# Two-expert mixture around linear attention: transpositions up to four items early in two PSUM banks, second products four items behind the first, bias and x sums behind the loop

## The chip, the cores and the metric

One core of one Trainium2 chip runs the whole program. Times are device microseconds of one execution. The kernel before took 328.78 us, the median of 3 runs (328.49 to 335.28).

## The reference

Input x is 2048 rows of 128 float32. The program computes

```
x = x + 0.5 * ffn(layernorm(x))
x = x + attention(layernorm(x))        # linear attention, 16 heads of 8, causal prefix sums
x = x + 0.5 * ffn(layernorm(x))

ffn(x):                                # 8 experts, 128 -> 512 -> 128, the best two per row
    logits = x @ Wg
    top_w, top_i = top_k(logits, 2);  top_w = softmax(top_w)
    for each expert i:
        h = gelu(x @ W1[i] + b1[i]);  out_i = h @ W2[i] + b2[i]
        results += weight_of_i_per_row * out_i
```

## The kernel before

All arithmetic on the matrices is float32. The program has three parts: a mixture of experts (pass f = 0), attention (tile by tile, 16 tiles of 128 rows), and a mixture again (pass f = 1). Each engine has its own instruction stream; semaphores order them. The change touches the mixture alone.

**Routing.** Each row has two (row, expert) pairs, 4096 in all. They are sorted by expert into 32 tiles (NL) of 128 slots. A tile that holds rows of two experts is worked on once for each, so there are at most NS = 32 + 8 - 1 = 39 "items". Tables in SBUF tell each item its tile (`place`), its expert (`expert_i`) and which lanes are its own (`own_item`).

**The expert loop.** For each item:

- POOL gathers the 128 rows of a tile from DRAM by an indirect DMA (line 411) into `xg`, which is the same memory as `y_back`. Gather n waits until transposition n - 6 is done (there are six semaphores, GATHERS). With a lag of 18 it scatters finished tiles to `y_rows` in DRAM (line 419) from the same queue: gather n, then scatter n - 18. Scatter i waits until item i + 7 is added up (`y_sb`).
- PE transposes the gathered rows (line 1090) into one PSUM bank, `xg_bank`; it waits for the gather and for ACT's copy of the transposition before. ACT copies it to SBUF (line 550) and clears the tile's sum (line 551).
- PE makes the first product (`hidden`, line 1072, 8 matmul instructions) of the expert's W1 and the turned rows into one of three banks. SP loads that expert's W1 and b1 (258 KB) into one of six buffers (WEIGHTS) once the item six before is done.
- DVE adds b1 (line 847) into one of three `h_pre`; ACT takes the GELU (line 558) into one of three `h_act`.
- PE makes the second product (`output`, line 1081, 8 matmul instructions) into one of three banks; it waits for the GELU and for DVE's sum of three items before. DVE adds it to the tile's sum for the lanes that are the item's own (line 859).

PE's order is written out by hand. Step i is: transposition i + 2, first product i + 1, (every second step) a register load of the next places, second product i - 1. PE's queue is in order, so each of these stands behind the one before. ACT's step i is: copy i + 2, clear, GELU i, and for 16 of the steps one diagonal of gate weights (line 561). DVE's step i is: bias add i, sum i - 2.

**Bias and x sums** (`mix_start`, lines 1111 and 1113). Four PSUM banks take, for four tiles each, the b2 of both experts by the row's weights (2 matmul instructions) and x itself through the identity (8). The one for c = 0 stands in PE's queue behind step 1, the other three behind the loop. Then the second product of the weighted rows (`mix`, line 1135) is added for each chunk as soon as SP has loaded it back from `y_rows`; DVE adds the row's other half into x (line 898).

In pass 0, DVE takes the moments of the new x behind this (line 892), and their variance goes through POOL (line 429) and DVE (lines 684 and 687) to ACT's first normalised tile of the attention (line 596).

Of the kernel before, what the change touches and what calls it, by code (L numbers as in the profile page):

```python
# [26 lines left out]
P = 128  # L27
# [10 lines left out]
def macaron_kernel(nc, x_d, xT_d, Wa, ba, Wg, W1b, W2, b2, out_d):  # L38
# [24 lines left out]
    PLACES = 2  # L63
    ITEM_STEPS = 21
    assert D == P and NS % RING == 0 and GATHERS % RING == 0 and WEIGHTS % RING == 0 and T & (T - 1) == 0

    with ExitStack() as ctx:
# [121 lines left out]
        h_act = sb("h_act", [P, RING, DF])  # L189
# [313 lines left out]
        def _(act):  # L503
            s = nc.scalar

            def ffn(f):
# [40 lines left out]
                def rows(n):  # L547

                    act.wait_ge(xg_ps, NL * f + n + 1)
                    s.copy(xgT[:, n * P:(n + 1) * P], xg_bank).then_inc(xg_sb, 1)  # L550
# [14 lines left out]
                step(0, 0)  # L565
                act.wait_ge(w_allT_ps, f + 1)
                s.copy(w_allT[:, :], w_allT_bank).then_inc(w_allT_sb, 1)
                step(1, 1)
                step(2, 2)
                act.wait_ge(half_ready, f + 1)  # L570
                for t in range(NT):
                    step(RING + t, t % RING)
                    weights(t)
                for i in range(RING + NT, NS):
                    step(i, i % RING, lead=(i + 2 < NL))
# [80 lines left out]
        def _(dve):  # L656
# [184 lines left out]
            def experts(f):  # L841
# [34 lines left out]
                for i in range(loops * WEIGHTS, NS + 2):  # L876
                    step(i, i % WEIGHTS)
# [95 lines left out]
        def _(pe):  # L973
# [70 lines left out]
            def experts(f):  # L1044
# [31 lines left out]
                def output(i, r):  # L1076
                    col = at[i][1]
                    pe.wait_ge(h_gelu, base + i + 1)
                    at_least(pe, y_sb, base + i - RING + 1)
                    for c in range(FC):  # L1080
                        last = mm(y_bank(r), h_act[:, r, c * P:(c + 1) * P], w2[:, bass.ds(col + c * P, P)],  # L1081
                                  start=(c == 0), stop=(c == FC - 1))
                    last.then_inc(y_ps, 1)

                def transposed_rows(n):

                    r = n % GATHERS
                    pe.wait_ge(gathered[r], 16 * (n // GATHERS + 1 + uses(r, GATHERS, NL) * f))
                    at_least(pe, xg_sb, NL * f + n)
                    pe.transpose(xg_bank, xg[:, n, :], ident[:, :]).then_inc(xg_ps, 1)  # L1090

                def step(i):

                    if i + 2 < NL:
                        transposed_rows(i + 2)
# [4 lines left out]
                    if i:  # L1100
                        output(i - 1, (i - 1) % RING)
# [17 lines left out]
                step(1)  # L1119
                if f == 0:  # L1120
# [159 lines left out]
```

## Time and profile before

| | us |
|---|---|
| median of 3 runs | 328.78 |
| lowest, highest | 328.49, 335.28 |
| span of the profiled execution | 363.5 |
| its own time | not given apart from the span |
| PE busy (matmuls) | 306.2 |
| PE weight loads busy | 253.4 |
| DVE busy | 206.9 |
| POOL busy | 192.9 |
| ACT busy | 152.1 |

The span runs from the first to the last instruction of one execution that the hardware profiler recorded. PE = matmul, PEld = its weight loads, DVE = VectorE, ACT = ScalarE, POOL = GpSimd, SP = SyncE. Matmul ends are modelled in it. "Remote", or "another core or an unknown queue", is what the profile writes where it can't name what ended a wait.

### The profile page before, as it was taken

How to read it: one execution, taken by the hardware profiler on the slowest of the kernel's cores; microseconds unless marked ns; L12 is line 12 of the kernel's file. 1: busy time of each engine (PE TensorE's matmuls, PEld its weight loads, DVE VectorE, ACT ScalarE, POOL GpSimd, SP SyncE). 2: the span in 40 equal slices, each digit the busy share in tenths (PEclk: the TensorE clock that was granted, in tenths of full speed). 3: DMA queues.
4: the chain of work that ended last, by engine and by line, in shares of the span. 5: the costliest groups of instructions: out<-in, count | busy, mean ns of one | idle time of the engine just before them, and what ended most of it. 6: DMA issues, size and time to landing. Idle time of an engine off the chain costs nothing.

```text
span 363.5 us, 7851 instructions
## 1 busy us (share of the span) xinstructions
PE 306.2 (84%) x2041; PEld 253.4 (70%) x2041; DVE 206.9 (57%) x558; ACT 152.1 (42%) x481; POOL 192.9 (53%) x246
## 2 busy tenths in 40 slices
PE   8785999686789986999999995868998577699975
PEld 6533899686779955566767763427998576699954
DVE  0896263423245416799999999992553323345504
ACT  1794475524244321434545551832664342343200
POOL 6056546666654531676677773236556665645610
PEclk9998999989899998999999998586999989989986
DMA  6937376445456116000000000236665543455156
GB/s 198 303 138 209 100 186 187 129 134 133 130 150 169 56 50 213 0 0 2 1 3 0 3 1 30 87 94 178 154 179 130 159 133 107 119 149 160 37 156 206
DMA packets 23557, 41.52 MB, mean 114 GB/s; under 512 B 4065, under 2 KB 6113, under 8 KB 23522
## 3 DMA queue, kind: packets, MB, share of 16 engines
q1 hardware_dynamic: 19426, 32.68, 32.0%
q0 software_dynamic: 4096, 8.40, 7.7%
q8 instruction: 19, 0.31, 0.3%
q14 instruction: 16, 0.13, 0.1%
HBM read 33.72 MB, written 7.34 MB: 113 GB/s over the span
## 4 chain that ended last, share of the span: by engine, by line
PE 47%; DVE 13%; another core or an unknown queue 12%; ACT 9%; issue 8%; DMA 7%; POOL 3%; SPq 0%; DVEq 0%; POOLq 0%; ACTq 0%
PE banks L1072 16%; PE banks L1081 14%; PE banks L1195 3%; DVE prod L927 3%; DVE local L931 3%; DMA y_back<-y_rows 3%; ACT h_act L558 2%; DMA y_back<-xn_rows,src_row 2%; PE banks L1090 2%; POOL kv L442 2%; PE banks L991 2%; PE banks L1135 2%; PE banks L980 2%; DMA y_rows<-y_back,pair_row 1%
## 5 line engine op out<-in xcount | busy, mean ns | idle before, releaser
L411 POOL DMA_INDIRECT y_back<-xn_rows,src_row x64 | 61.9, 967 | 61.6 <-issue 21.7
L1072 PE MATMUL banks<-rows_sb,w1b 128*128 x624 | 91.0, 292 | 1.2 <-issue 1.2
L847 DVE TENSOR_TENSOR h_pre<-banks,w1b 128x512 f32<-128x512 f32 x78 | 53.7, 688 | 64.3 <-PE banks L1072 41.6
L1081 PE MATMUL banks<-w,h_act 128*128 x624 | 85.4, 283 | 1.1 <-ACT h_act L558 1.1
L1072 PEld LDWEIGHTS banks<-rows_sb,w1b 128*128 128x128 f32 x624 | 82.3, 205 | 3.6 <-issue 1.9
L419 POOL DMA_INDIRECT y_rows<-y_back,pair_row x64 | 62.6, 978 | 39.8 <-DVE y_back L859 22.9
L1081 PEld LDWEIGHTS banks<-w,h_act 128*128 128x128 f32 x624 | 79.0, 199 | 1.3 <-issue 1.3
L558 ACT ACTIVATE h_act<-h_pre 128x512 f32<-128x512 f32 x78 | 48.7, 624 | 22.1 <-DVE h_pre L847 17.4
L859 DVE SCALAR_TENSOR_TENSOR y_back<-banks,own_item,y_back 128x128 f32 x78 | 27.4, 351 | 51.4 <-PE banks L1081 32.1
L550 ACT COPY rows_sb<-banks 128x128 f32<-128x128 f32 x64 | 16.8, 262 | 85.4 <-remote 54.2
L1090 PE MATMUL banks<-ident,y_back 128*128 128x128 f32 x64 | 19.3, 302 | 28.2 <-issue 12.3
L442 POOL TENSOR_TENSOR kv<-qk,vx 128x1024 f32<-128x1024 f32 x16 | 31.5, 1969 | 18.1 <-DVE qk L884 18.1
L1090 PEld LDWEIGHTS banks<-ident,y_back 128*128 128x128 f32 x64 | 9.8, 153 | 32.2 <-issue 25.2
L1195 PE MATMUL banks<-kv,tri 128*128 128x384 f32 x64 | 24.8, 509 | 2.3 <-POOL kv L442 2.3
L980 PE MATMUL banks<-blank 128*128 128x512 bf16 x65 | 23.2, 524 | 1.2 <-DVE blank L915 1.2
L927 DVE TENSOR_TENSOR prod<-banks,qk 128x1152 f32<-128x1152 f32 x16 | 21.6, 1351 | 2.0 <-PE banks L1199 1.4
L931 DVE TENSOR_REDUCE local<-prod 128x144 f32<-128x1152 f32 x16 | 21.6, 1353 | 0.6
L898 DVE SCALAR_TENSOR_TENSOR x<-y_back,half_w,banks 128x128 f32<-128x128 f32 x32 | 8.9, 342 | 20.3 <-PE banks L1135 11.3
L551 ACT ACTIVATE y_back<-ident 128x128 f32<-128x128 f32 x64 | 20.1, 314 | 0.0
L1195 PEld LDWEIGHTS banks<-kv,tri 128*128 128x128 f32 x64 | 10.9, 189 | 9.7 <-POOL kv L442 5.3
L1135 PE MATMUL banks<-y_back,diag 128*128 128x128 f32 x64 | 12.5, 372 | 5.3 <-DMA y_back<-y_rows 5.3
L980 PEld LDWEIGHTS banks<-blank 128*128 128x128 bf16 x65 | 7.7, 126 | 12.9 <-issue 8.4
(201 smaller groups left out, 427.1 us busy)
## 6 DMA issues: line engine op xcount, KB each, us to landing
w1b<-in_W1b SPq DMA_DIRECT2D x78, 258.0 KB
y_back<-y_rows SPq DMA_DIRECT2D x16, 256.0 KB, 5.6
xn_rows<-rows_sb SPq DMA_DIRECT2D x8, 256.0 KB, 2.3
rows_sb<-in_x_T SPq DMA_DIRECT2D x4, 256.0 KB, 4.0
x<-in_x_tiles SPq DMA_DIRECT2D x4, 256.0 KB, 6.2
y_back<-xn_rows,src_row POOLq DMA_INDIRECT x64
y_rows<-y_back,pair_row POOLq DMA_INDIRECT x64
out<-x SPq DMA_DIRECT2D x4, 256.0 KB, 2.3
```

Source lines behind the costliest of these rows:

```text
L411: g.indirect_dma_start(out=xg[:, n, :], out_offset=None, in_=xn_rows[f][:, :], in_offset=bass.IndirectOffsetOnAxis(ap=src_row[:, n:n + 1], ...
L419: g.indirect_dma_start(out=y_rows[f][:, :], out_offset=bass.IndirectOffsetOnAxis(ap=pair_row[:, i:i + 1], axis=0), in_=xg[:, i, :], in_off ...
L442: g.tensor_tensor(o4, k4, v4, ALU.mult).then_inc(kv_sb, 1)
L558: s.activation(h_act[:, r, :], h_pre[:, r, :], ACT.Gelu_apprx_tanh).then_inc(h_gelu, 1)
L847: v.tensor_tensor(h_pre[:, r, :].rearrange("p (c n) -> p c n", c=FC), h_bank(r).rearrange("p (c n) -> p c n", c=FC), w1b[:, q, DF:DF + FC] ...
L927: v.tensor_tensor(prod[:, :].rearrange("p (b e n) -> p b e n", b=3, n=P), prefix_bank.rearrange("p b (e n) -> p b e n", n=P), q4, ALU.mult ...
L931: v.tensor_reduce(local[:, :, :].rearrange("p e h -> p (e h)"), prod[:, :].rearrange("p (g d) -> p g d", d=DH), AX.X, ALU.add).then_inc(lo ...
L980: mm(banks[:, bank, :], blank[:, 0:P], blank[:, :], start=True, stop=True)
L1072: last = mm(h_bank(r)[:, c * P:(c + 1) * P], w1b[:, q, c * P:(c + 1) * P], xgT[:, bass.ds(at[i][0], P)], start=True, stop=True)
L1081: last = mm(y_bank(r), h_act[:, r, c * P:(c + 1) * P], w2[:, bass.ds(col + c * P, P)], start=(c == 0), stop=(c == FC - 1))
L1090: pe.transpose(xg_bank, xg[:, n, :], ident[:, :]).then_inc(xg_ps, 1)
L1195: mm(prefix_bank[:, b, :], tri[:, :], kv[:, r, b * n:(b + 1) * n, :].rearrange("p e n -> p (e n)"), start=True, stop=True)
```

## The change

The transpositions alternate between two PSUM banks (0 and 1). A function `turned(i)` says how many tiles are transposed by the end of step i: i + 3 as before, one more from step 3 and two more from step 6, at most 32. PE and ACT both follow it. The second product of item i - 3 stands in step i, where that of i - 1 stood; `h_act` has six buffers in place of three. DVE's sum moves from i - 2 to i - 4. The transposed gate weights move from bank 1 to bank 7. All four `mix_start` stand behind the last second product.

```diff
+    TURNS = 2
+    BEHIND = 3
+    AHEAD = 4
+    ACTS = 6
...
-        h_act = sb("h_act", [P, RING, DF])
+        h_act = sb("h_act", [P, ACTS, DF])
...
-        xg_bank = banks[:, 0, 0:P]
+        def xg_bank(n): return banks[:, n % TURNS, 0:P]
+        def turned(i):
+            return min(i + 3 + min(max(i, 0) // 3, AHEAD - 2), NL)
...
-        w_allT_bank = banks[:, 1, 0:P]
+        w_allT_bank = banks[:, 7, 0:P]
...
-                def step(i, r, lead=True):
-                    if lead:
-                        rows(i + 2)
+                def step(i):
+                    for n in range(turned(i - 1), turned(i)):
+                        rows(n)
                     act.wait_ge(h_biased, base + i + 1)
-                    at_least(act, y_ps, base + i - RING + 1)
-                    s.activation(h_act[:, r, :], h_pre[:, r, :], ACT.Gelu_apprx_tanh).then_inc(h_gelu, 1)
+                    at_least(act, y_ps, base + i - ACTS + 1)
+                    s.activation(h_act[:, i % ACTS, :], h_pre[:, i % RING, :], ACT.Gelu_apprx_tanh).then_inc(h_gelu, 1)
...
-                    if not isinstance(i, int) or i >= 2:
-                        output(i - 2, (q - 2) % RING)
+                    if not isinstance(i, int) or i > BEHIND:
+                        output(i - BEHIND - 1, (q - BEHIND - 1) % RING)
...
-                    at_least(pe, xg_sb, NL * f + n)
-                    pe.transpose(xg_bank, xg[:, n, :], ident[:, :]).then_inc(xg_ps, 1)
+                    at_least(pe, xg_sb, NL * f + n - TURNS + 1)
+                    pe.transpose(xg_bank(n), xg[:, n, :], ident[:, :]).then_inc(xg_ps, 1)
                 def step(i):
-                    if i + 2 < NL:
-                        transposed_rows(i + 2)
+                    for n in range(turned(i - 1), turned(i)):
+                        transposed_rows(n)
                     if i + 1 < NS:
                         hidden(i + 1)
                     if i + 2 < NS and (i + 2) % PLACES == 0:
                         places(i + 2)
-                    if i:
-                        output(i - 1, (i - 1) % RING)
+                    if i >= BEHIND:
+                        output(i - BEHIND)
...
                 step(1)
+                step(2)
+                pe.wait_ge(w_allT_sb, f + 1)
+                for i in range(3, NS):
+                    step(i)
+                for i in range(NS - BEHIND, NS):
+                    output(i)
                 if f == 0:
                     pe.wait_ge(b2_in, 16)
-                pe.wait_ge(w_allT_sb, f + 1)
-                mix_start(0)
-                for i in range(2, NS):
-                    step(i)
-                output(NS - 1, (NS - 1) % RING)
-                for c in range(1, NC):
+                for c in range(NC):
                     mix_start(c)
```

## Rows read from the trace of the kernel before

**Rows 1.** The page: busy time by engine, and the clock in 40 slices.
```profile
PE 306.2 (84%) x2041; PEld 253.4 (70%) x2041; DVE 206.9 (57%) x558; ACT 152.1 (42%) x481; POOL 192.9 (53%) x246
...
PEclk9998999989899998999999998586999989989986
```

**Rows 2.** The chain in order of time: start us, us, what.
```profile
29.03 3.71 DMA y_back<-xn_rows,src_row
...
57.99 0.89 PE banks L1072 x8
58.89 0.89 PE banks L1081 x8
...
96.34 5.60 another core or an unknown queue
...
140.00 2.09 PE banks L1135 x8
...
241.60 3.54 DMA y_back<-xn_rows,src_row
```

**Rows 3.** Timeline of PE in the first loop, 53.9 to 62.6 us.
```profile
54.93 1.06 PE L1081 MATMUL banks<-w,h_act 128*128 x8
...
57.72 0.27 PE L1090 MATMUL banks<-ident,y_back 128*128 128x128 f32 x1
57.83 1.06 PE L1072 MATMUL banks<-rows_sb,w1b 128*128 x8
...
59.62 0.27 PE L1090 MATMUL banks<-ident,y_back 128*128 128x128 f32 x1
...
61.62 1.06 PE L1072 MATMUL banks<-rows_sb,w1b 128*128 x8
```

**Rows 4.** First products (L1072) by stretch: length, PE, PEld, clock, DMA, GB/s.
```profile
61.60:106.45 44.85, 18.04 (x120) 16.03 (x121) 0.92 0.48 131
275.10:319.20 44.10, 16.23 (x112) 14.44 (x113) 0.94 0.46 129
```

**Rows 5.** Timeline of POOL, 57 to 75 us.
```profile
58.27 0.94 POOL L411 DMA_INDIRECT y_back<-xn_rows,src_row  x1 [0.95 <-PE banks L1090]
59.52 1.01 POOL L419 DMA_INDIRECT y_rows<-y_back,pair_row  x1 [0.30 <-issue]
60.83 0.97 POOL L411 DMA_INDIRECT y_back<-xn_rows,src_row  x1 [0.30 <-issue]
```

**Rows 6.** Timeline of the first loop's start, 26 to 46 us.
```profile
40.08 1.12 PE L1111 MATMUL banks<-b_blk,w_allT 32*128 32x512 f32 x2
...
42.13 0.27 PE L1090 MATMUL banks<-ident,y_back 128*128 128x128 f32 x1
```

**Rows 7.** The waits of the whole span: us in total, times, longest.
```profile
ACT rows_sb L550 <- remote: 54.2, 15, 5.6
...
PE banks L1090 <- ACT rows_sb L550: 11.5, 7, 3.3
```

**Rows 8.** Timeline behind the first loop, 124 to 150 us.
```profile
128.55 1.15 PE L1081 MATMUL banks<-w,h_act 128*128 x8 [1.11 <-ACT h_act L558]
...
131.12 0.97 POOL L419 DMA_INDIRECT y_rows<-y_back,pair_row  x1 [0.30 <-issue]
131.77 1.12 PE L1111 MATMUL banks<-b_blk,w_allT 32*128 32x512 f32 x2
...
133.91 1.12 PE L1111 MATMUL banks<-b_blk,w_allT 32*128 32x512 f32 x2
...
137.46 1.13 PE L1135 MATMUL banks<-y_back,diag 128*128 128x128 f32 x8 [1.35 <-DMA y_back<-y_rows]
...
140.00 3.63 PE L1135 MATMUL banks<-y_back,diag 128*128 128x128 f32 x16 [1.41 <-DMA y_back<-y_rows]
...
143.16 0.15 DVE L684 SCALAR_TENSOR_TENSOR shift<-mean,rstd 128x4 f32<-128x4 f32 x1
```

**Rows 9.** Timeline behind the second loop, 339 to 364 us.
```profile
354.71 4.68 PE L1135 MATMUL banks<-y_back,diag 128*128 128x128 f32 x24 [1.14 <-DMA y_back<-y_rows]
```

More of the change, by code:

```diff
@@ L63, in macaron_kernel @@
     PLACES = 2
+    TURNS = 2
+    BEHIND = 3
+    AHEAD = 4
+    ACTS = 6
     ITEM_STEPS = 21
-    assert D == P and NS % RING == 0 and GATHERS % RING == 0 and WEIGHTS % RING == 0 and T & (T - 1) == 0
+    assert D == P and NS % RING == 0 and GATHERS % RING == 0 and WEIGHTS % RING == 0 and WEIGHTS % ACTS == 0 and T & (T - 1) == 0
     with ExitStack() as ctx:
@@ L549, in rows @@
                     act.wait_ge(xg_ps, NL * f + n + 1)
[L550 removed]
+                    s.copy(xgT[:, n * P:(n + 1) * P], xg_bank(n)).then_inc(xg_sb, 1)
                     s.activation(y_sum[:, n * P:(n + 1) * P], ident[:, :], ACT.Copy, scale=0.0).then_inc(zeroed, 1)
[L553 to L555 removed]
+                def step(i):
+                    for n in range(turned(i - 1), turned(i)):
+                        rows(n)
                     act.wait_ge(h_biased, base + i + 1)
[L557 to L558 removed]
+                    at_least(act, y_ps, base + i - ACTS + 1)
+                    s.activation(h_act[:, i % ACTS, :], h_pre[:, i % RING, :], ACT.Gelu_apprx_tanh).then_inc(h_gelu, 1)
                 def weights(t):
@@ L564, in ffn @@
                 rows(1)
-                step(0, 0)
+                step(0)
                 act.wait_ge(w_allT_ps, f + 1)
                 s.copy(w_allT[:, :], w_allT_bank).then_inc(w_allT_sb, 1)
-                step(1, 1)
-                step(2, 2)
+                step(1)
+                step(2)
                 act.wait_ge(half_ready, f + 1)
                 for t in range(NT):
-                    step(RING + t, t % RING)
+                    step(RING + t)
                     weights(t)
                 for i in range(RING + NT, NS):
-                    step(i, i % RING, lead=(i + 2 < NL))
+                    step(i)
                 if f == 0:
@@ L875, in experts @@
                         step(j * WEIGHTS + q, q)
-                for i in range(loops * WEIGHTS, NS + 2):
+                for i in range(loops * WEIGHTS, NS + BEHIND + 1):
                     step(i, i % WEIGHTS)
@@ L1074, in hidden, with output @@
                     last.then_inc(h_ps, 1)
-                def output(i, r):
-                    col = at[i][1]
+                def output(i):
+                    col, r, a = at[i][1], i % RING, i % ACTS
                     pe.wait_ge(h_gelu, base + i + 1)
@@ L1080, in output @@
                     for c in range(FC):
-                        last = mm(y_bank(r), h_act[:, r, c * P:(c + 1) * P], w2[:, bass.ds(col + c * P, P)],
+                        last = mm(y_bank(r), h_act[:, a, c * P:(c + 1) * P], w2[:, bass.ds(col + c * P, P)],
                                   start=(c == 0), stop=(c == FC - 1))
@@ L1119, in experts @@
                 step(1)
+                step(2)
+                pe.wait_ge(w_allT_sb, f + 1)
+                for i in range(3, NS):
+                    step(i)
+                for i in range(NS - BEHIND, NS):
+                    output(i)
                 if f == 0:
                     pe.wait_ge(b2_in, 16)
-                pe.wait_ge(w_allT_sb, f + 1)
-                mix_start(0)
-                for i in range(2, NS):
-                    step(i)
-                output(NS - 1, (NS - 1) % RING)
-                for c in range(1, NC):
+                for c in range(NC):
                     mix_start(c)
```

## The prediction

> **What bounds the kernel now.** I read the page's first two parts, then the chain in order of time, then the two expert loops (the two passes f = 0 and f = 1 of the mixture of experts), which hold some 200 of the 363.5 us, engine by engine, and last the stretch behind each loop. The reader is to see first that PE is the busiest engine and is granted nearly its full clock [rows 1]. In the chain the loops are an unbroken run of "0.89 PE" pieces, twice per item (once for each product), but with a stretch in the middle of each loop where pieces of 4 to 6 us appear under "another core or an unknown queue" [rows 2]. So each loop has two regimes.
>
> In the free regime PE has no gap: transposition, first product and second product start 1.90 us after those of the item before (57.72 to 59.62), which is 0.11 for the transposition and 0.89 for each product [rows 3]. The transposition never waits for ACT's copy there, nor the second product for the GELU. In the other regime, from 61.60 to 106.45 in pass one and from 275.10 to 319.20 in pass two, 15 and 14 items (120 and 112 matmuls by eight) take 44.85 and 44.10 us, that is 3.0 to 3.15 each [rows 4]. At 1.90 they would take 28.5 and 26.6. The excess is 16.35 + 17.5 = 33.9 us.
>
> Now the profiled span against the timed runs: 363.5 - 33.9 = 329.6, and the median is 328.78. I have no separate time of the profiled execution beside its span, so whatever lies around the span is in this difference of 0.8 too. My reading is that the timed executions run both loops at the free pace, and the slow stretch belongs to the profiled one. I therefore work with a "free" frame: the trace's times, with the items after number 13 moved forward to 1.90 each, so that the last second product of pass one, which ends at 129.70 (128.55 + 1.15), ends at about 112.2 (129.70 - 16.4 - 1.1, the last being a wait for a late GELU, L1081 in [rows 8], that pass two doesn't have), and its last scatter, which starts at 131.12, starts at about 113.5 [rows 8].
>
> **POOL, the second engine.** It issues 64 indirect DMAs per pass in one queue: 18 gathers, then pairs of gather and scatter, then 18 scatters. Busy time is 0.94 to 1.01 each, but starts are 1.25 to 1.31 apart, so a pair takes 2.56 (58.27 to 60.83, [rows 5]). That is more than PE's 1.90 per item. The Trainium skill (Perfetto Trace Analysis, GPSIMD Engine Instruction) says that such spans are unreliable and that start-to-start spacing is what to time by; by the busy time of 0.97 a pair would cost 1.94 and never be late, by the spacing it is late as worked out below. The trace agrees: the 0.30 between two of them stands in every row. What keeps POOL from being late now is a lead: gather n is released by transposition n - 6, and in the free regime POOL idles 0.95 per gather for it (58.27 in [rows 5]).
>
> **The change, part by part.**
>
> (a) *Bias and x sums for the first four tiles behind the loop.* Removed from the loop: 2 + 8 matmuls, from 40.08 to where the next transposition starts, 42.13, so 2.05 us, 2.1 with its share of pipeline [rows 6]. Behind the loop it is repeated as a fourth block of 2.14 (131.77 to 133.91 for one block, [rows 8]). There PE has 1.35 us of idle time before the first mixing product at 137.46 and 1.41 before the second at 140.00 [rows 8]. So PE gains 2.1 per loop and the cover behind the loop is short by 2.14 - 1.35 = 0.8 for the first chunk alone; the second and later chunks wait for their loads anyway.
>
> (b) *Second products four items behind.* The order of PE's queue changes, not its content: three second products instead of one stand behind the last first product. At any given first product PE has done two second products less, so items come 2 x 0.89 = 1.8 earlier and their results 2 items later. Since PE has no gap in the free regime, this wins nothing there. It removes the 1.1 us wait before the last second product, where there is one. Scatter i waits for item i + 7, so POOL's first scatter moves.
>
> (c) *Transpositions up to two items further ahead, in two banks.* The wait for ACT's copy cost PE 11.5 us over the whole trace, the copies themselves waiting for "remote" 54.2 [rows 7]; all but a little of it is in the slow stretches, so it is worth about 0 in the free frame (bounds 0 and 11.5). But a transposition stands in PE's in-order queue and waits for its gather. Behind it are queued the first products of items already turned and all second products that are due. The gather is now wanted sooner: number 31 was wanted at 61.62 + 17 x 1.90 = 93.9. Now it is wanted two items (3.8) earlier, less 2.1 from (a), less 1.8 from (b): 86.2.
>
> (d) *POOL against PE.* A gather lands 3.5 to 3.7 after its start (29.03 and 241.60 in [rows 2]). Before: gather 19 starts at 60.83 and gather 31 twelve pairs later, at 91.5 with 2.56 per pair, landing at 95.1: PE is 1.2 late. After: the first scatter, now at 59.52, waits for item 7, whose second product comes at 54.93 - 2.1 + 1.8 = 54.6, so it starts near 56.5, gather 19 near 57.8, gather 31 at 88.5, landed at 92.0, where PE wants it at 86.2: 5.8 late. PE's loop then ends at 112.2 - 2.1 + 5.8 = 115.9 instead of 113.4. The end of the pass is set by the last scatter. Before, that is POOL's own line: 92.8 + 18 x 1.28 = 115.8. After, the last four second products come 0.89 apart, faster than POOL's 1.28: item 35 is added up at 115.9 - 2.7 + 0.4 = 113.6, and the last scatter starts three places later, at 117.4. Sum per pass at this pace: +1.6.
>
> How certain is 1.28? With it the old kernel's last scatter would start at 115.8 and not 113.5, and the timed run would be some 2 x 2.3 longer than 329.6; it is not. So POOL is probably a little faster unprofiled. At 1.20 (pair 2.40): before, last scatter 113.5; after, gather 31 at 86.6, landed 90.1, 3.9 late, loop end 114.0, last scatter 115.3: +1.8. At 1.10: gather 31 at 84.2, landed 87.7, 1.5 late, loop end 111.6, last scatter 112.6 against 113.3: -0.7. At 1.0 and below, no lateness: -2.1. The ends are -2.1 and +1.8 per pass; I take the mean of 1.28, 1.20 and 1.10: (1.6 + 1.8 - 0.7) / 3 = +0.9, so +1.8 for two passes.
>
> (e) *The clock behind the loop.* The eight products at 140.00 take 2.09 and the 24 at 354.71 take 4.68, against 0.89 per eight at the full clock: this is the lower level of 1.2 GHz, after PE had idled [rows 2, 8, 9]. PE is now busy 2.1 longer in front of them. If the clock stays up, 1.2 in pass one and 2.0 in pass two are won; if not, nothing. Against that stand the 0.8 of (a), which in pass one reach the chain through the variance and the shift at 143.16 [rows 8]. I take half the gain: -1.6 + 0.8 = -0.8.
>
> Six GELU buffers instead of three, a second PSUM bank and the moved bank for the transposed weights add no instruction. SP's weight loads are released by the first products and their bias adds, which come earlier by the same amount as PE. Sum: 328.8 + 1.8 - 0.8 = 329.8. The limit of what the measurement can tell is about 2%, 6.6 us.
>
> **The rivals.**
>
> *R1, the slow stretch is partly in the timed runs too, and the longer distances hide it.* For: in it PE idles while ACT's copy, DVE's add and POOL's gather all wait on PE's signals, and both the second bank and the four places are what would bridge such a delay; the highest of the three runs, 335.28, leaves room for 6. Against: 329.6 meets 328.78 without it. If a quarter of 33.9 is there and goes: 328.8 - 8.5 = 320. Chance 0.16.
>
> *R2, POOL's queue becomes the bound: slower.* The mechanism is (d), at the place of transpositions 22 to 31. It decides from a start-to-start pace of about 1.15; at 1.28, with gathers landing a microsecond later than in the rows since scatters now run beside them from sooner on, it is 1.6 + 1.0 = 2.6 per pass. With PE idle about 0.65 of 2.56 in each item the granted clock can fall, as it did in the slow stretch (0.92, [rows 4]); an eight-matmul product at the low level costs 0.8 more, two or three falls per pass some 2 us. Together 328.8 + 5.2 + 4 - 0.8 = 337. For: the spacing in the rows. Against: the timed run. Chance 0.15 (two thirds of it beyond 2%).
>
> *R3, PE's shortening arrives.* POOL at 1.0 to 1.1 and the clock stays up behind the loop: 328.8 - 4.2 - 3.2 + 0.8 = 322. Chance 0.14.
>
> *R4, the change doesn't do what it says:* if PE's queue waits at the gathers, the rows are turned no earlier than now. That is part of R2 and of my forecast, at no time of its own.
>
> **How the numbers follow.** Forecast 0.55, R1 0.16, R2 0.15, R3 0.14. The forecast's own range is 326 to 333. For 8 in 10 the range takes in R3 and about half each of R2 and R1: 321 to 335.5. Faster by over 2% (below 322.2): most of R1 and a fifth of R3, 0.17. Slower by over 2% (above 335.4): 0.10. Within: 0.73.
>
> **What would show it.** In the new trace: (1) no bias or x sums among the first loop items and four blocks behind the loop; (2) in the free regime items still 1.90 apart: this is the step on which "no gain" rests; (3) the transposition rows between the twentieth and the last show PE waiting for "DMA y_back<-xn_rows", where they now show none; (4) the last scatter starts within 2 us of where it would have in the free frame; (5) mixing products of eight at 0.9 to 1.1 behind the loop if (e) holds. I am wrong if the slow stretches vanish from the trace and the time falls with them (R1), or if a wait for gathers of over 6 us per pass stands in it (R2).

## The result and the profile after

The changed kernel takes 336.66 us, the median of 4 runs (333.56 to 339.32), against 328.82 of the kernel before (328.49 to 335.28): a ratio of 1.0188, interval 1.0097 to 1.028. Repeated later, beside another 17 runs of the kernel before, it is 1.0221 (1.014 to 1.0303). So it is about 2% slower, with both intervals above 1 and reaching to either side of 2%. Every ratio here compares only the executions in the faster of two states in which each kernel runs, so it is not the quotient of the medians, which hold all runs. I had forecast 329.8, at most a slight loss.

The execution behind the new profile took 335.03 us, of which 333.2 are the span. The page, against [rows 1]:

```profile
span 333.2 us, 7837 instructions
...
PE 289.5 (87%) x2036; PEld 238.5 (72%) x2041; DVE 209.1 (63%) x558; ACT 152.8 (46%) x481; POOL 193.2 (58%) x246
...
PEclk9589799999999999999999999677999999999998
```

The span is 30 us shorter than that of [rows 1], though the kernel is slower. The stretches of "another core or an unknown queue" of [rows 2] are gone, and they are in none of the twelve traces taken later, those of the kernel before among them. A fair comparison needs such a trace, so I took another one of the kernel before (run `base`, 327.8 us, span 325.9) and use it from here on.

PE's timeline in the first loop of the changed kernel, which answers to [rows 3]. Transposition 25 is the one at 75.69, number 31 that at 91.24:

```profile
75.69 0.33 PE L1101 MATMUL banks<-ident,y_back 128*128 128x128 f32 x1 [0.29 <-DMA y_back<-xn_rows,src_row]
75.89 1.15 PE L1083 MATMUL banks<-rows_sb,w1b 128*128 x8
76.88 1.06 PE L1092 MATMUL banks<-w,h_act 128*128 x8
77.81 0.33 PE L1101 MATMUL banks<-ident,y_back 128*128 128x128 f32 x1
...
80.19 0.33 PE L1101 MATMUL banks<-ident,y_back 128*128 128x128 f32 x1
...
84.03 0.33 PE L1101 MATMUL banks<-ident,y_back 128*128 128x128 f32 x1 [1.59 <-DMA y_back<-xn_rows,src_row]
...
91.24 0.33 PE L1101 MATMUL banks<-ident,y_back 128*128 128x128 f32 x1 [1.18 <-DMA y_back<-xn_rows,src_row]
```

From 75.69 to 91.24 the six transpositions are 1.9 to 3.8 apart, on the mean 2.59 and not 1.90: PE goes at the pace of the gathers, 2.57. POOL at the same time, which answers to [rows 5]; L422 is a gather, L430 a scatter:

```profile
50.25 0.94 POOL L422 DMA_INDIRECT y_back<-xn_rows,src_row  x1 [0.30 <-issue]
55.29 1.01 POOL L430 DMA_INDIRECT y_rows<-y_back,pair_row  x1 [4.09 <-DVE y_back L870]
56.60 0.98 POOL L422 DMA_INDIRECT y_back<-xn_rows,src_row  x1 [0.30 <-PE banks L1101]
...
84.84 0.97 POOL L422 DMA_INDIRECT y_back<-xn_rows,src_row  x1 [0.30 <-issue]
86.11 0.99 POOL L430 DMA_INDIRECT y_rows<-y_back,pair_row  x1 [0.30 <-issue]
87.40 0.97 POOL L422 DMA_INDIRECT y_back<-xn_rows,src_row  x1 [0.30 <-issue]
...
112.11 0.97 POOL L430 DMA_INDIRECT y_rows<-y_back,pair_row  x1 [0.82 <-DVE y_back L870]
113.38 0.97 POOL L430 DMA_INDIRECT y_rows<-y_back,pair_row  x1 [0.30 <-issue]
...
117.20 0.97 POOL L430 DMA_INDIRECT y_rows<-y_back,pair_row  x1 [0.30 <-issue]
```

Three things stand here. POOL idles 4.09 us before scatter 0, for the later result of item 7. Then pairs follow each other every 2.57 without a gap, so the gathers are as fast as this queue can be. At the end scatters wait for DVE again (0.82), so the last items are late for POOL. The same places in the kernel before (`base`; L411 gather, L419 scatter):

```profile
55.06 0.94 POOL L411 DMA_INDIRECT y_back<-xn_rows,src_row  x1 [0.95 <-PE banks L1090]
56.31 1.01 POOL L419 DMA_INDIRECT y_rows<-y_back,pair_row  x1 [0.30 <-issue]
57.62 0.97 POOL L411 DMA_INDIRECT y_back<-xn_rows,src_row  x1 [0.30 <-issue]
...
111.34 0.97 POOL L419 DMA_INDIRECT y_rows<-y_back,pair_row  x1 [0.30 <-issue]
112.62 0.97 POOL L419 DMA_INDIRECT y_rows<-y_back,pair_row  x1 [0.30 <-issue]
```

There POOL never waits from scatter 0 to the last one: 56.31 + 44 operations of 1.28 = 112.6. The whole waits, changed kernel and kernel before:

```profile
POOL y_rows L430 <- DVE y_back L870: 25.1, 28, 4.1
...
PE banks L1101 <- DMA y_back<-xn_rows,src_row: 13.1, 11, 3.0
```

```profile
PE banks L1090 <- DMA y_back<-xn_rows,src_row: 5.8, 5, 1.9
POOL y_rows L419 <- DVE y_back L859: 4.0, 13, 0.3
```

Where the 7.3 us between the two spans (333.2 - 325.9) are, counted from the start of gather 0 of each pass: the last scatter starts at 89.9 instead of 85.5 in pass one (+4.4) and at 89.0 instead of 85.4 in pass two (+3.6). From there to gather 0 of pass two it is 109.6 against 109.75, and to the end 17.4 against 18.1: -0.8 together. Gather 0 itself starts 0.1 later (27.29 against 27.15). Between these two traces all of the loss is in the two loops. They are one execution each, and executions of one kernel differ by as much (`base2` below), so the runs below test each part.

### The profile page after: what moved, and what is told of

The parts are those of the page before. It is cut to its first block, busy times and chain, and to the rows that moved or that the text cites. A ratio compares the mean times of both kernels' runs of the same rounds, so it can differ in the third digit from the quotient of the medians.

```text
span 333.2 us, 7837 instructions
## 1 busy us (share of the span) xinstructions
PE 289.5 (87%) x2036; PEld 238.5 (72%) x2041; DVE 209.1 (63%) x558; ACT 152.8 (46%) x481; POOL 193.2 (58%) x246
## 4 chain that ended last, share of the span: by engine, by line
PE 48%; DVE 13%; DMA 12%; POOL 11%; issue 9%; ACT 4%; SPq 1%; POOLq 0%; DVEq 0%; ACTq 0%
PE banks L1083 15%; PE banks L1092 15%; DMA y_back<-xn_rows,src_row 8%; POOL y_rows L430 4%; POOL y_back L422 4%; PE banks L1206 4%; DVE prod L938 3%; DVE local L942 3%; DMA y_back<-y_rows 2%; PE banks L1101 2%; POOL kv L453 2%; PE banks L991 2%; PE banks L1182 2%; PE banks L1124 1%; ACT rows_sb L596 1%
## 5 line engine op out<-in xcount | busy, mean ns | idle before, releaser
L1083 PE MATMUL banks<-rows_sb,w1b 128*128 x624 | 86.5, 283 | 1.2 <-ACT rows_sb L561 0.5
L430 POOL DMA_INDIRECT y_rows<-y_back,pair_row x64 | 62.7, 979 | 37.3 <-DVE y_back L870 25.1
L422 POOL DMA_INDIRECT y_back<-xn_rows,src_row x64 | 62.0, 969 | 36.4 <-issue 26.3
L1092 PE MATMUL banks<-w,h_act 128*128 x624 | 81.1, 275 | 0.0
L1083 PEld LDWEIGHTS banks<-rows_sb,w1b 128*128 128x128 f32 x624 | 78.0, 197 | 3.1 <-issue 2.2
L1092 PEld LDWEIGHTS banks<-w,h_act 128*128 128x128 f32 x624 | 75.3, 192 | 0.0
L1101 PE MATMUL banks<-ident,y_back 128*128 128x128 f32 x64 | 18.7, 298 | 13.5 <-DMA y_back<-xn_rows,src_row 13.1
L991 PE MATMUL banks<-blank 128*128 128x512 bf16 x60 | 20.9, 506 | 2.1 <-DVE blank L926 1.2
L1101 PEld LDWEIGHTS banks<-ident,y_back 128*128 128x128 f32 x64 | 9.3, 146 | 17.8 <-DMA y_back<-xn_rows,src_row 17.4
L607 ACT ACTIVATE xa<-x,shift,rstd 128x128 f32<-128x128 f32 x16 | 8.0, 505 | 15.7 <-DVE shift L698 15.7
```

The costliest lines, as they stand in the source:

```text
L422: g.indirect_dma_start(out=xg[:, n, :], out_offset=None, in_=xn_rows[f][:, :], in_offset=bass.IndirectOffsetOnAxis(ap=src_row[:, n:n + 1], ...
L430: g.indirect_dma_start(out=y_rows[f][:, :], out_offset=bass.IndirectOffsetOnAxis(ap=pair_row[:, i:i + 1], axis=0), in_=xg[:, i, :], in_off ...
L991: mm(banks[:, bank, :], blank[:, 0:P], blank[:, :], start=True, stop=True)
L1083: last = mm(h_bank(r)[:, c * P:(c + 1) * P], w1b[:, q, c * P:(c + 1) * P], xgT[:, bass.ds(at[i][0], P)], start=True, stop=True)
L1092: last = mm(y_bank(r), h_act[:, a, c * P:(c + 1) * P], w2[:, bass.ds(col + c * P, P)], start=(c == 0), stop=(c == FC - 1))
L1101: pe.transpose(xg_bank(n), xg[:, n, :], ident[:, :]).then_inc(xg_ps, 1)
```

## The experiments

Twelve runs follow the changed kernel's first one. The table holds what the timelines of the traces show for each pass, in us after gather 0: start of scatter 0, gather 31 and transposition 31; the products of eight matmuls that stand behind transposition 31 in PE's queue, first and second ones together; the end of the last of them; the start of the last scatter.

| run | pass | scatter 0 | gather 31 | transp. 31 | products behind | PE's end | last scatter |
|---|---|---|---|---|---|---|---|
| base | 1 / 2 | 29.15 / 29.1 | 61.3 / 61.2 | 64.7 / 64.7 | 20 | 82.95 / 83.0 | 85.5 / 85.4 |
| changed | 1 / 2 | 28.0 / 27.8 | 60.1 / 60.0 | 63.95 / 63.2 | 26 | 87.6 / 86.7 | 89.9 / 89.0 |
| after_again | 1 / 2 | 28.45 / 28.9 | 60.55 / 61.1 | 63.9 / 64.35 | 26 | 87.6 / 88.0 | 89.9 / 90.3 |
| a_ahead2 | 1 / 2 | 26.8 / 28.5 | 58.9 / 60.6 | 62.5 / 63.7 | 22 | 82.6 / 83.8 | 84.9 / 86.1 |
| a_behind1 | 1 / 2 | 26.9 / 24.9 | 59.0 / 57.0 | 62.4 / 60.1 | 24 | 84.3 / 82.0 | 85.85 / 83.5 |
| a_lag22 | 1 / 2 | 31.8 / 30.5 | 53.6 / 52.4 | 58.4 / 57.2 | 26 | 81.9 / 80.7 | 84.2 / 82.95 |
| b_lag22 | 1 / 2 | 39.05 / 36.5 | 60.9 / 58.4 | 65.7 / 64.0 | 20 | 83.8 / 82.3 | 90.3 / 87.7 |
| b_mix | 1 / 2 | 29.1 / 29.1 | 61.2 / 61.2 | 64.5 / 64.5 | 20 | 82.9 / 82.8 | 85.4 / 85.4 |
| b_mix2 | 1 / 2 | 26.7 / 26.8 | 58.8 / 58.9 | 62.55 / 62.25 | 20 | 80.9 / 80.6 | 83.0 / 83.2 |
| b_warm | 1 / 2 | 29.0 / 28.85 | 61.1 / 61.0 | 64.4 / 64.4 | 20 | 82.75 / 82.75 | 85.3 / 85.3 |
| base2 | 1 / 2 | 31.7 / 29.0 | 63.8 / 61.2 | 67.3 / 64.5 | 20 | 85.5 / 82.8 | 88.1 / 85.4 |
| a_b1_lag20 | 1 / 2 | 27.8 / 28.6 | 54.8 / 55.6 | 58.3 / 59.0 | 24 | 80.1 / 80.7 | 81.6 / 82.4 |
| a_b1_lag20_warm | 1 / 2 | 29.8 / 27.0 | 56.75 / 54.0 | 60.4 / 57.5 | 24 | 82.3 / 79.2 | 83.8 / 80.8 |

And the times. The kernel before was run beside each of the three groups:

| run | us, median | before beside it | ratio, 95% |
|---|---|---|---|
| a_ahead2 | 328.98 | 333.63 | 0.9897, 0.9639 to 1.0155 |
| a_behind1 | 327.34 | 333.63 | 0.9883, 0.9827 to 0.9938 |
| a_lag22 | 325.13 | 333.63 | 0.9861, 0.9722 to 0.9999 |
| after_again | 337.68 | 332.56 | 1.0221, 1.0140 to 1.0303 |
| b_lag22 | 338.09 | 332.56 | 1.0201, 1.0105 to 1.0296 |
| b_mix | 327.92 | 332.56 | 0.9880, 0.9831 to 0.9929 |
| a_b1_lag20 | 323.34 | 332.56 | 0.9810, 0.9741 to 0.9879 |
| b_warm | 329.10 | 331.74 | 0.9941, 0.9902 to 0.9981 |
| a_b1_lag20_warm | 322.81 | 331.74 | 0.9734, 0.9680 to 0.9788 |
| base, base2, b_mix2 | 327.8, 335.71, 321.22 | | one execution each |

Of the 16 runs of the kernel before beside the last group one took 638.1 us, the others 328.95 to 334.79. Nothing here explains it.

**base: the kernel before, no edit.**

> The kernel before once more, for a profile in which the loops may run without the slow stretch, as they do in the profile of the changed kernel. Theory (POOL's pairs of gather and scatter, 2.57 us against PE's 1.90 per item, are late only when the rows are wanted early): transpositions wait for gathers under 1.5 us per pass between items 19 and 31, the last scatter of pass one starts some 86 to 88 us after the first gather (changed kernel: 89.9). Rival (the gathers are late in the kernel before as well, and the loss is elsewhere, behind the loop): waits of 4 us per pass here too.

Of the 5.8 us that PE waits for gathers in the whole span most lies at the loops' starts; at the end of pass one PE comes 1.3 us late (from transposition 28 at 84.85 to 31 at 91.86 it is 7.0 where three items take 5.7). The last scatter starts at 85.5, where the theory had 86 to 88. So the kernel before is already a little late on gathers, but it doesn't matter there: POOL's own line ends later than PE's results (its last product ends at 110.1, the last scatter starts at 112.6). The rival falls.

**a_ahead2: rows no earlier than before.**

```diff
-    AHEAD = 4
+    AHEAD = 2
```

> The changed kernel with AHEAD = 2, so that step i transposes tile i + 2 as before; two banks, second products four behind, sums behind the loop all stay. Theory (rows wanted two items sooner than POOL can bring them): they are wanted 3.8 us later, the waits of PE for gathers fall from 4.3 to about 1 us per pass, the time by 4 to 7 us, to 328 to 331. Rival one (late results from the second products cost the time): no change from the changed kernel, 335. Rival two (the sums behind the loop): no change either.

328.98, as the theory had it; PE's waits for gathers are 6.1 us in the whole span instead of 13.1, and the last scatter starts 5.0 and 2.9 earlier than in the changed kernel. The ratio's interval is wide and doesn't tell this kernel from the kernel before; but five of its six runs are below the fastest of the changed kernel's (333.56), and the traces' loops agree. So turning two items further ahead is needed for the loss.

**a_behind1: second products two items behind, as before.**

```diff
-    BEHIND = 3
+    BEHIND = 1
```

> The changed kernel with BEHIND = 1, second products two items behind the first as before; the rest stays, rows four ahead. Theory: scatter 0 is released 3.8 us sooner, POOL's pairs start sooner, and every first product comes 1.8 us later, so the rows are at most 1 us late: 327 to 331. Rival one (late results at the loop's end): also faster, 331, but with PE's waits for gathers unchanged at 4 us per pass. Rival two (sums behind the loop): 335.

327.34; the waits are 7.4 instead of 13.1, and POOL's idle time before scatter 0 is 1.36 instead of 4.09:

```profile
55.94 1.01 POOL L430 DMA_INDIRECT y_rows<-y_back,pair_row  x1 [1.36 <-DVE y_back L870]
...
112.34 0.97 POOL L430 DMA_INDIRECT y_rows<-y_back,pair_row  x1 [0.82 <-DVE y_back L870]
...
114.88 0.97 POOL L430 DMA_INDIRECT y_rows<-y_back,pair_row  x1 [0.30 <-issue]
```

So the second part is needed for the loss as well: with it taken back the kernel is 1.2% faster than before (0.9827 to 0.9938). This and the run before it make the loss one of the two together. Beside part (a) alone (`b_mix` below, 0.9880) the ratios stay where they were with one of the two added, 0.9897 and 0.9883, and only with both is it 1.0188.

**a_lag22: four more gathers ahead of the first scatter.**

```diff
-                lag = 18
+                lag = 22
```

> The changed kernel with a lag of 22 instead of 18 between gather and scatter in POOL's queue; nothing else. Theory: POOL stood idle 4 us before scatter 0 and now issues four more gathers there and ahead of the pairs; gather 31 starts at about 81 us instead of 87.4 in pass one, no transposition waits, PE's loop ends 4.5 us sooner per pass: 325 to 328, faster than both kernels. Rivals (late results, sums behind the loop): 335, as neither depends on POOL's order.

325.13, and the trace's span is 322.0. POOL around scatter 0: the gathers fill what was idle time, and gather 31 starts at 53.6 after gather 0 instead of 60.1.

```profile
55.40 0.94 POOL L422 DMA_INDIRECT y_back<-xn_rows,src_row  x1 [0.96 <-PE banks L1101]
57.30 0.94 POOL L422 DMA_INDIRECT y_back<-xn_rows,src_row  x1 [0.95 <-PE banks L1101]
58.54 1.01 POOL L430 DMA_INDIRECT y_rows<-y_back,pair_row  x1 [0.30 <-issue]
```

From 60 to 90 us no wait of PE for a gather is left in the list of waits; in the changed kernel 4.7 stand there from 60 to 93, where its last one ends. PE's content, its 26 products behind transposition 31 and the sums behind the loop are unchanged, so the rivals that put the loss there fall: what cost the time is when the gathers land.

**after_again: the changed kernel once more.**

> The changed kernel once more, beside the variants on one chip. Theory, from the traces so far: PE ends a loop of pass one when gather 31 has landed (64.0 us after gather 0) and the 26 products that stand behind transposition 31 are through (23.3): 87.4 to 87.8, and the last scatter starts 2.3 later, at 89.9. Time 334 to 339. Rival (the first trace was an odd one): 328 to 331, with the last scatter before 87.

337.68, and both passes again at 89.9 and 90.3. The first products of pass one run at the full clock, as in `base`, and not partly at the lower one as in the changed kernel's first trace; so the clock at the loop's start is not what separates 89.9 from 85.5:

```profile
33.48 1.15 PE L1083 MATMUL banks<-rows_sb,w1b 128*128 x8 [0.54 <-ACT rows_sb L561]
...
36.15 1.15 PE L1083 MATMUL banks<-rows_sb,w1b 128*128 x8
```

**b_lag22: the same lag in the kernel before.**

```diff
-                lag = 18
+                lag = 22
```

> The kernel before with a lag of 22 in POOL's queue; nothing else. Theory (in the kernel before, POOL's own line sets the last scatter: start of scatter 0 plus 44 operations of 1.28): gathers 19 to 21 are released by transpositions 13 to 15, so scatter 0 starts 5 us later, at 34.6 after gather 0 instead of 29.2, and only 41 operations follow: last scatter at 87.1 against 85.5, slower by 1.6 per pass, 3 us in all, though PE never waits for a gather. Rival (PE's waits for gathers set the time of the kernel before too): faster by 1.3 per pass.

Slower by 2%, with the sign of the theory and twice its size: it said 3 us, and the ratio gives some 6.6. The last scatter starts at 90.3 and 87.7, 4.8 and 2.3 later than in `base`. POOL's line holds to 0.1: scatter 0 at 39.05 plus 40 operations of 1.28 is 90.25. What I had missed is that scatter 0 stands behind gather 22, not 21, and that pass one began at the lower clock (first products of 2.07), which pass two didn't. POOL's timeline where the scatters begin:

```profile
64.95 0.94 POOL L411 DMA_INDIRECT y_back<-xn_rows,src_row  x1 [0.95 <-PE banks L1090]
66.85 0.94 POOL L411 DMA_INDIRECT y_back<-xn_rows,src_row  x1 [0.95 <-PE banks L1090]
68.09 1.01 POOL L419 DMA_INDIRECT y_rows<-y_back,pair_row  x1 [0.31 <-issue]
```

The last gathers ahead of the first scatter go at PE's 1.90 and leave POOL idle for 0.95 each. Four more of them delay scatter 0 by 4 x 1.90 = 7.6 and leave four operations fewer behind it, 5.1: 2.5 later by this, and 2.3 in pass two. The gathers come sooner than in `base` there, and yet the kernel is slower: so the old kernel isn't bound by PE's waits for gathers but by POOL's own line. The same edit takes the changed kernel from 2.2% slower than the kernel before to 1.4% faster (ratios 1.0221 and 0.9861), and makes this one 2% slower.

**b_mix: the first part alone, in the kernel before.** The bias and x sums of the first block leave the loop and are done behind it; the distances stay.

```diff
-                if f == 0:
-                    pe.wait_ge(b2_in, 16)
...
-                mix_start(0)
...
-                for c in range(1, NC):
+                if f == 0:
+                    pe.wait_ge(b2_in, 16)
+                for c in range(NC):
```

> The kernel before with only part (a) of the change: all four blocks of bias and x sums behind the loop. Theory: transpositions come 2.1 us sooner, with them gathers 10 to 18 and item 7, so scatter 0 and POOL's whole line start 2.1 sooner: last scatter 83.4 after gather 0, time 4 us less than before, 324 to 326 where the kernel before takes 327.8. Rival (POOL's line does not hang on PE's start, or the blocks behind the loop cost as much as they save there): within 1 us of the kernel before.

Faster, 0.9880, which is 4.0 us. But the trace does not show how, for its last scatters start at 85.4, as in `base`. The reason stands at the start of the loop, in PE's timeline of `b_mix` and then of `base`:

```profile
32.27 2.07 PE L1072 MATMUL banks<-rows_sb,w1b 128*128 x8 [0.54 <-ACT rows_sb L550]
...
35.25 2.05 PE L1072 MATMUL banks<-rows_sb,w1b 128*128 x8
```

```profile
32.19 1.15 PE L1072 MATMUL banks<-rows_sb,w1b 128*128 x8 [0.55 <-ACT rows_sb L550]
...
34.21 1.15 PE L1072 MATMUL banks<-rows_sb,w1b 128*128 x8
```

In this execution of `b_mix` the first products ran at the lower clock, which put scatter 0 where `base` has it without the sums. So two executions of different kernels differ in the edit and in the clock at the loop's start. `base` itself, 327.8 where the 17 runs of the same kernel beside it have a median of 333.63 (327.44 to 335.86), was at the fast end. I took this as a theory for the next group: another trace of each kernel should show the last scatter at scatter 0 plus 56.3, wherever the clock puts scatter 0.

**base2: the kernel before once more.** No edit.

> The kernel before, one more profile. Open since the last runs: its one undisturbed trace took 327.8 and its median beside it 332 to 333. Theory (the granted clock falls at the loops' start in some executions and not in others; in that trace it didn't): an execution of 331 or more shows the first three first products of a pass at 1.6 to 2.1 us instead of 1.1, scatter 0 later than 29.2 after gather 0, and the last scatter later than 85.5 by as much. Rival (the 4 us lie elsewhere): the loops measure the same, 85.5.

335.71. In the first pass the second and third first product are at the lower clock:

```profile
33.67 1.19 PE L1072 MATMUL banks<-rows_sb,w1b 128*128 x8 [0.54 <-ACT rows_sb L550]
...
36.10 1.99 PE L1072 MATMUL banks<-rows_sb,w1b 128*128 x8
...
38.32 1.92 PE L1072 MATMUL banks<-rows_sb,w1b 128*128 x8
```

Scatter 0 starts at 31.7 and the last at 88.1 in pass one, 2.6 later than in pass two, which starts at the full clock (29.0 and 85.4). The rest of the 8.0 us between the two spans is 3.9 behind the loop of pass one, from the last scatter to gather 0 of pass two (113.7 against 109.75), and 1.9 ahead of gather 0 (29.03 against 27.15); the end takes 0.4 less. Neither of these two is explained by the loops. So the same kernel can take as long as the changed one did in its first trace (333.9 against 333.2): the loss is seen in the medians and in the loops of both traces of each kernel, not in one pair of spans.

**b_mix2: `b_mix` once more.** No further edit.

> The kernel with part (a) alone, one more profile. In its first trace the last scatter started 85.4 after gather 0, as in the kernel before, though the median was 1.2% better; its first products ran at the low clock. Theory: in a pass that starts at the full clock the last scatter starts at 83.4. Rival: at 85.4 in any case.

321.22. Both passes start at the full clock (1.15 per product of eight), and now the part shows alone: scatter 0 at 26.7 and the last scatter at 83.0 and 83.2, which is 2.4 and 2.3 earlier than in `base`. Another 1.6 us of the span are saved behind the second loop, which one execution cannot assign. POOL's scatter 0 waits in each pass for nothing but its own queue, and what follows goes at 1.28 to the end:

```profile
53.77 1.01 POOL L419 DMA_INDIRECT y_rows<-y_back,pair_row  x1 [0.30 <-issue]
...
110.11 0.97 POOL L419 DMA_INDIRECT y_rows<-y_back,pair_row  x1 [0.30 <-issue]
```

56.34 us for 44 operations: 1.280 each. The 2.05 us of PE's time in the loop come out as POOL's line starting 2.3 to 2.5 earlier.

**a_b1_lag20: the changed kernel with two of its numbers set for POOL's queue.** Second products two items behind, and two more gathers ahead of the first scatter.

```diff
-    BEHIND = 3
+    BEHIND = 1
...
-                lag = 18
+                lag = 20
```

> The changed kernel with BEHIND = 1 and a lag of 20. Theory: rows four ahead let POOL gather sooner, scatter 0 is released by item 7 at 26 us, two more gathers go in front of the pairs, transposition 31 never waits, PE's loop ends near 81 and the last scatter starts at 83 to 84: the best of all, 322 to 325. Rival (the second products four behind are what wins in the variant with a lag of 22): slower than that one, 327 or more.

323.34, 0.9810 (0.9741 to 0.9879), faster than both kernels. POOL idles 0.95 us before the last gather ahead of scatter 0, for a transposition, and not at all before scatter 0 itself:

```profile
55.79 0.94 POOL L422 DMA_INDIRECT y_back<-xn_rows,src_row  x1 [0.95 <-PE banks L1101]
57.03 1.01 POOL L430 DMA_INDIRECT y_rows<-y_back,pair_row  x1 [0.30 <-issue]
```

The last scatter is at 27.8 + 42 x 1.28 = 81.6, which the table has (I had expected 83 to 84), and PE's last product ends at 80.1: here both lines end together (see the table below). No wait of PE for a gather is left between 60 and 92 us.

**b_warm: more idle matmuls ahead of the loop, in the kernel before.** They compute nothing that is used; there are 13 instead of 8 in that place.

```diff
-    WARM_COUNTS, WARM_HOTS, WARM_INVERSE, WARM_EXPERTS, WARM_PREFIX = 8, 4, 4, 8, 8
+    WARM_COUNTS, WARM_HOTS, WARM_INVERSE, WARM_EXPERTS, WARM_PREFIX = 8, 4, 4, 13, 8
```

> The kernel before with five more idle-filling matmuls ahead of the first transposition (13 instead of 8). Theory (PE's pause of 1.6 to 2.6 us before the first rows land lets the clock fall in some executions, which costs 2 us at each loop's start): median 328 to 330 instead of 332 to 333. Rival (the clock's fall has its cause further back, or the extra matmuls delay the first transposition): 332 or more.

329.10, 0.9941 (0.9902 to 0.9981): a small gain, with the median in the range expected, and its trace has both last scatters at 85.3 and both passes at the full clock, as `base` has without the added matmuls. The 12 runs still go from 326.5 to 334.5, and one trace can't tell whether the clock at the loop's start is what the gain comes from.

**a_b1_lag20_warm: the same in `a_b1_lag20`.**

> The variant with BEHIND = 1 and a lag of 20, with the same five more matmuls. Theory: its rows come early enough that PE's start sets its loops, so it gains too, 320 to 322 against 323.3 without. Rival: 323 or more.

322.81, 0.9734 (0.9680 to 0.9788), the lowest median of all, though not the 320 to 322 expected. The interval overlaps that of `a_b1_lag20`, so a gain of the added matmuls of their own is not shown here; in its trace pass one has its last scatter 3.0 later than pass two (83.8 against 80.8), with scatter 0 2.8 later.

**Two lines that end a loop.** The table gives them both. POOL's line: the last scatter starts at scatter 0 plus 44, 42 or 40 operations of 1.28, for a lag of 18, 20 or 22. PE's line: its last product ends at transposition 31 plus the products behind it times 0.893, plus 0.3 to 0.5, and then the scatters that are left. The last second products come 0.89 apart behind the last first product, three of them in the kernel before and five in the changed one:

```profile
107.26 2.85 PE L1081 MATMUL banks<-w,h_act 128*128 x24
```

```profile
110.29 4.63 PE L1092 MATMUL banks<-w,h_act 128*128 x40
```

(`base`, then the changed kernel.) The scatters that wait for their results go at 1.28, so the last of them starts 1.5 us after PE's end where second products are two items behind and 2.3 where they are four behind. The 1.5 is read from `a_behind1`, where POOL waits for DVE's sum at 112.34 and has the last scatter two places on (114.88), and the 2.3 from the changed kernel. The last scatter is the later of the two lines.

| run, pass one | POOL's line | PE's end + 1.5 or 2.3 | measured |
|---|---|---|---|
| base | 85.5 | 84.5 | 85.5 |
| base2 | 88.0 | 87.0 | 88.1 |
| b_mix2 | 83.0 | 82.4 | 83.0 |
| b_lag22 | 90.3 | 85.3 | 90.3 |
| changed | 84.3 | 89.9 | 89.9 |
| a_ahead2 | 83.1 | 84.9 | 84.9 |
| a_lag22 | 83.0 | 84.2 | 84.2 |
| a_behind1 | 83.2 | 85.8 | 85.85 |
| a_b1_lag20 | 81.6 | 81.6 | 81.6 |
| a_b1_lag20_warm | 83.6 | 83.8 | 83.8 |

(PE's line by the measured end of its last product.) In the kernel before POOL's line ends last, with PE's only 1.0 us ahead of it. The change pulls PE's products forward, and with them POOL's line by 1.2, but puts six more products (5.4 us) behind transposition 31, and transposition 31 comes only 0.75 earlier, since gather 31 starts only 1.2 earlier. 5.4 - 0.75 = 4.6, and PE's end is 87.6 instead of 82.95. With 0.8 more for the scatters behind it, less the 1.0 us of room, that makes the 4.4 of pass one.

## Why the prediction was off

The forecast was 329.8, the measurement is 1.0188 times 328.8, or 335.0 by that ratio and 336.66 as measured. The range for 8 in 10, 321 to 335.5, holds the first of these by half a microsecond and not the second; that it comes this near is owed to the width of the range and not to the sum. The mechanism that I had in step (d), and in its strong form as R2, is the one that happened; what failed was its size, +0.9 per pass where it was +4.4 and +3.6.

**Step (d), the pace.** It had the terms for both paces and then took a mean of three, +0.9 per pass, on the argument that 1.28 did not fit the timed run. Measured: wherever POOL doesn't wait between scatter 0 and the last one it goes at 1.28 (pairs of 2.57), in every trace read. The argument failed because its frame was wrong. "363.5 - 33.9 = 329.6, and the median is 328.78" compares a trace mended by calculation with a median; a trace without the slow stretches has a span of 325.9 for an execution of 327.8 (the same 1.9 added to 329.6 gives 331.5, not 328.78), and the executions of this kernel go up to 335, in part with the clock at the start of the loops (`base2`). So there were some microseconds of room in the median which I used to argue POOL's pace away. By the rule of the Trainium skill (Perfetto Trace Analysis, GPSIMD Engine Instruction), which I had cited and then softened, the spacing is the time: the traces agree, 0.97 busy and 1.28 from start to start.

**Step (d), the size at 1.28.** It had +1.6 per pass at that pace; measured are +4.4 and +3.6. Counted from gather 0 (which was at 29.03 in the trace that I worked from), the two ends are off in opposite directions:

- Before: forecast 115.8 - 29.0 = 86.8, measured 85.5. Gather 19 was read from the first trace as 31.8 after gather 0; in `base` it is 30.5. The first trace began this pass partly at the lower clock (first products of 1.83 and 1.60, in `base` 1.15), and so did `base2`, where the last scatter is at 88.1. That PE comes 1.2 late at transposition 31 of the kernel before was right: 1.3 in `base`.
- After: forecast 117.4 - 29.0 = 88.4, measured 89.9. Gather 31 lands 3.84 after its start (87.40 to 91.24) and not 3.5, transposition 31 is at 63.95 and not 63.0, and the last scatter is 2.3 behind PE's end and not 1.5, since five second products end the loop and not four.

1.3 + 1.5 = 2.8 is the whole gap between +1.6 and +4.4 in pass one.

**Step (b).** "This wins nothing there" holds, but it costs: each place that the second products are moved behind puts one more product behind transposition 31 and lets POOL stand idle longer before scatter 0 (4.09 against 1.36 in `a_behind1`). The forecast had this in the end of the loop as part of (d) and never priced the step alone. `a_behind1` does: 4.1 and 5.5 per pass between its last scatters and those of the changed kernel. Of this 1.8 are two products and 0.8 the scatters behind them; the rest is transposition 31, 1.5 and 3.1 earlier with POOL's earlier scatter 0.

**Step (c).** Right that it wins nothing at the free pace: where no gather is awaited the transpositions are 1.90 apart, and PE waits for no copy. Right too that it makes PE want its gathers sooner. `a_ahead2` prices it at 5.0 and 2.9 per pass. Both prices are for a part beside the other one, and don't add up: the loss is theirs together.

**Step (a).** Right in sign and size: PE wins 2.05 in the loop, and the last scatter comes 2.3 to 2.4 earlier in `b_mix2`. Behind the loop the four blocks run without a gap into the mixing, as the chain of the changed kernel in order of time shows:

```profile
114.92 1.05 PE banks L1122 x2
115.97 1.09 PE banks L1124 x8
...
122.39 1.09 PE banks L1124 x8
123.48 0.91 PE banks L1146 x8
```

**Step (e).** Forecast -0.8, found -0.8 between two traces, with the first mixing products of eight in the chain at 0.91 instead of 2.09, and a granted clock of 1.00 instead of 0.93 from 112 to 135 us. But `base` and `base2` differ by 4 us in that stretch with the same code, so the match shows nothing: that the clock stays up is seen, what it is worth stays open.

**The rivals.** R1: the slow stretches are gone from the new trace, but from those of the kernel before too, and the time did not fall. No trace but the first has them, though the other executions take as long as the timed runs do; so nothing points to them in the timed runs. R2 happened, with 4.0 per pass (mean of 4.4 and 3.6) where it had 2.6, and without its fall of the clock. Its 337 meets the measured 336.66 by luck: 2 x 1.4 us too little for the gathers and 4 us for a clock that didn't fall. PE's busy time and granted clock in both waiting stretches, as windows of the changed kernel's trace show them:

```profile
272.00:291.00 19.00, 16.00 (x128) 14.78 (x128) 7.65 (x15) 7.65 (x24) 14.43 (x16) 1.00 0.52 147
64.00:92.00 28.00, 23.20 (x193) 21.86 (x193) 11.82 (x23) 12.19 (x39) 21.30 (x22) 1.00 0.59 165
```

The columns are the window, its length, the busy time of PE, PE's weight loads, DVE, ACT and POOL, PE's clock, and the share of the DMA engines and their GB/s. PE is idle for 3.0 and 4.8 us there, and its clock stays at 1.00.

R3 fell with the pace. R4's mechanism, the queue waiting at the gathers, is in R2. Of the five signs, the first three and the fifth were there (the third with 13.1 us in 11 waits, 7.6 in pass one and 5.5 in pass two, of which part is at the loops' starts; R2's own sign, over 6 us per pass, was thus met in pass one alone); the fourth was not, as the last scatter came at 89.9 and not within 2 us of the 84.5 (113.5 - 29.0) of the free frame.

**Still open.** What made the slow stretches in the first trace; why the clock is low at a loop's start in some executions; what made the 638.1 us of one run; and why the transposition that waits for a gather starts 3.0 us after the gather in one place (gather 30 in pass two of `a_ahead2`) and 4.4 in another (gather 29 in pass two of the changed kernel). None was tried on its own, apart from `b_warm` for the clock. The second PSUM bank wasn't tried on its own either; in `base` the wait that it takes away is 0.4 us in the whole span.

## What to carry to other kernels

In an in-order queue, fetching a thing earlier helps only if the feeder can deliver earlier. If it can't, the consumer waits at the same place as before, and all work that was reordered to stand behind that place is added to the end: count the items behind the last awaited arrival and multiply by their price, before and after. The loop grows by that less the room which this queue had before another line ended last. Where a second queue alternates two kinds of work, look at where the second kind begins first, since here a lag of 22 with the new order won 1.4% against the kernel before (20, with second products two items behind, 1.9%), where the same order with 18 lost 2%, and 22 with the old order lost 2% as well. When a trace has stretches that the timed runs don't have, take a new trace before working from a mended one.

## What the runs showed of the hardware that I had not expected

- POOL's indirect DMAs (128 rows each) start 1.28 us apart, first gathers and scatters in turn and then scatters alone, on the mean of 40 to 44 in a row (56.31 us for 44 in `base`, 56.34 in `b_mix2`, 51.21 for 40 in `b_lag22`), with a busy time of 0.94 to 1.01.
- The granted clock at the start of a loop differs between executions of one kernel: the first products of eight take 1.15 or about 2.0 us, that is the level of 2.4 or of 1.2 GHz. In `base2` the pass that starts lower has its last scatter 2.6 later than the other, and one execution of the kernel before took 327.8, another 335.7.
- The first profiled execution held some 33.9 us in slow stretches [rows 4], and none of the later traces has them.
